# Order of work in a unit of the second attention: q in two halves, transposes and scores between the products

## What is computed

```python
kv = concat([context, latents], axis=1)          # 64 + 256 = 320 keys a batch
q = (latents @ Wq).reshape(bsz, q_len, 32, 128)  # 32 query heads
k, v = kv @ Wk, kv @ Wv                          # 8 key/value heads, 4 query heads to each
q, k = rms_norm(q, q_norm_w), rms_norm(k, k_norm_w)
scores = einsum('bhgqd,bhkd->bhgqk', qg, k) / sqrt(128)
out = einsum('bhgqk,bhkd->bhgqd', softmax(scores), v)
x = x + tanh(g_xattn[1]) * (out @ Wo)            # latents = layernorm(x)
```

## Time and profile before

| | us |
|---|---|
| median of three runs | 1485.03 (1480.28 to 1485.92) |
| the profiled execution | 1481.86 |
| its span, first to last instruction | 1480.1 |
| of it the 32 units of the second attention | 552.4 to 1412.3 |
| PE busy | 1394.9 (94%) |
| DVE busy | 1055.5 (71%) |
| ACT busy | 799.7 (54%) |
| POOL busy | 464.1 (31%) |

### The profile page before, as it was taken

The page is one execution under the profiler, slowest core; times in us unless marked ns, Lnnn a source line. Parts: engine busy times, 40 slices in busy tenths (PEclk is TensorE's granted clock), DMA queues, the critical chain, the costliest instruction groups (busy, mean ns, idle before and its releaser), DMA issues.

```text
span 1480.1 us, 24307 instructions
## 1 busy us (share of the span) xinstructions
PE 1394.9 (94%) x7976; PEld 1197.7 (81%) x7976; DVE 1055.5 (71%) x2794; ACT 799.7 (54%) x2210; POOL 464.1 (31%) x590
## 2 busy tenths in 40 slices
PE   4999999998999998999999999999999999999988
PEld 4888888897778877888878878878888888887777
DVE  7777777778632437787777777787787787787775
ACT  4777777776211315565555555555555555664642
POOL 3855555554963612111111111111121111112220
PEclk8999999999999999999999999999999999999999
DMA  4211212111321301001001001001001001010001
GB/s 192 72 62 53 71 71 71 59 69 44 105 68 43 124 1 72 1 1 72 1 1 71 0 1 71 0 1 71 0 1 71 0 1 71 0 43 13 1 8 50
DMA packets 14958, 63.96 MB, mean 43 GB/s; under 512 B 1760, under 2 KB 1760, under 8 KB 10656
## 3 DMA queue, kind: packets, MB, share of 16 engines
q1 hardware_dynamic: 14880, 63.07, 12.0%
HBM read 60.97 MB, written 2.10 MB: 43 GB/s over the span
## 4 chain that ended last, share of the span: by engine, by line
PE 39%; DVE 15%; issue 5%; ACT 4%; DVEq 0%; ACTq 0%
PE psum L57 12%; PE psum L59 11%; PE psum L58 11%; PE psum L1356 2%; PE psum L1450 2%; DVE mx L1041 2%; DVE pT_hi L1014 2%; DVE pT_lo L1010 1%; DVE w1o_lo L1003 1%; DVE p L1056 1%; DVE w1q_lo L1003 1%; ACT pT_hi L1212 1%; DVE dump L1034 1%; DVE oT_lo L1020 1%; DVE v_lo L1071 1%
## 5 line engine op out<-in xcount | busy, mean ns | idle before, releaser
L1289 ACT ACTIVATE p<-psum,nb,rq 128x320 f32<-128x320 f32 x256 | 155.2, 613 | 162.8 <-DVE nb L1045 162.8
L57 PE MATMUL psum<-w1q_hi,xnT_lo 128*128 128x512 f32 x288 | 120.9, 420 | 16.7 <-DVE v_lo L1065 9.0
L978 POOL TENSOR_TENSOR rk<-ssk,rms_eps 128x3 f32<-128x3 f32 x32 | 6.3, 196 | 350.7 <-DVE ssk L1082 350.7
L59 PE MATMUL psum<-w1q_hi,xnT_hi 128*128 128x512 f32 x288 | 113.7, 395 | 0.0
L1010 DVE TENSOR_TENSOR pT_lo<-psum,pT_hi 128x512 fp32r<-128x512 f32 x128 | 88.1, 689 | 35.9 <-ACT pT_hi L1212 34.1
L58 PE MATMUL psum<-w1q_lo,xnT_hi 128*128 128x512 f32 x288 | 112.9, 392 | 0.0
L1041 DVE TENSOR_REDUCE mx<-psum 128x2 f32<-128x640 f32 x128 | 105.0, 820 | 6.1 <-PE psum L59 0.5
L1253 ACT ACTIVATE q_raw<-psum 128x512 f32<-128x512 f32 x64 | 38.2, 597 | 123.6 <-PE psum L59 123.6
L363 DVE TENSOR_TENSOR VW_lo<-psum,VW_hi 64x512 fp32r<-64x512 f32 x128 | 88.0, 688 | 19.0 <-ACT VW_hi L459 17.4
L57 PE MATMUL psum<-w1o_hi,oT_lo 128*128 128x512 f32 x256 | 100.5, 393 | 0.0
L58 PE MATMUL psum<-w1o_lo,oT_hi 128*128 128x512 f32 x256 | 100.3, 392 | 0.0
(11 more groups left out here) (235 smaller groups left out, 4657.6 us busy)
## 6 DMA issues: line engine op xcount, KB each, us to landing
raw_q<-in_w0q SPq DMA_DIRECT2D x8, 1024.0 KB, 4.8
raw_o<-in_w0o SPq DMA_DIRECT2D x8, 1024.0 KB, 4.8
raw_q<-in_w1q SPq DMA_DIRECT2D x8, 1024.0 KB, 7.5
raw_o<-in_w1o SPq DMA_DIRECT2D x8, 1024.0 KB, 4.8
raw_kv<-in_w_gu SPq DMA_DIRECT2D x10, 512.0 KB, 3.6
raw_gu<-in_w_gu SPq DMA_DIRECT2D x10, 512.0 KB, 3.7
raw_kv<-in_w0kv SPq DMA_DIRECT2D x8, 515.0 KB, 3.3
raw_kv<-in_w1kv SPq DMA_DIRECT2D x8, 512.0 KB, 5.5
```

Source lines behind the costliest of these rows:

```text
L57: pe.matmul(out, w[1], m[0], start=start, stop=False)
L59: return pe.matmul(out, w[0], m[0], start=False, stop=stop)
L1289: last = act.activation(k.p1[:, tile, h, :], s_pair(j)[:, h % 2, :], ACT.Exp, bias=k.nb[:, i:i + 1], scale=k.rq[:, i:i + 1], accum_out=k.r ...
```

## The change

It moves work in the streams of PE, DVE and ACT, and changes two shapes:

- **q in halves by pairs of heads.** `q_proj(n, b, hp)` makes both token tiles of one pair of heads into one bank: 24 instructions of 256 columns for each half, 48 in place of 24 of 512. `q_raw` and `qT` hold the halves so; transposes, squares and splits keep their number and sizes.
- **PAIRS** goes through both tiles of heads 0 and 1 first, then of heads 2 and 3.
- **Transposes of p:** groups 0 to 2 (first pair of heads) stand in the unit itself, after score steps 2 and 3; groups 3 to 5 stay in the next unit. `p_v` comes ahead of q there.
- **Splits of weights** (`pieces`): all of `w1o` in b = 1; in b = 3 all six pieces, at new places.
- The layer-norm tiles for later phases (`ln_tiles`) and the tail follow the new order.

```diff
-    PAIRS = [(0, 0), (0, 1), (1, 0), (1, 1)]
+    PAIRS = [(0, 0), (1, 0), (0, 1), (1, 1)]
...
-        order = ["kv"] + (["cx"] if b % 2 == 0 else []) + ["q0", "q1", "pv0", "pv1", "d0", "d1"]
+        order = ["kv"] + (["cx"] if b % 2 == 0 else []) + ["pv0", "q0", "q1", "pv1", "d0", "d1"]
...
+        order = ["t3", "t4", "k", "t5", "q0", "q1", "t0", "t1", "t2"]
...
+            def q_proj(n, b, hp):
+                for tile in range(2):
+                    t = 2 * b + tile
+                    for c in range(CH):
+                        last = mm3(pe, y_bank(b, "q", hp)[:, tile * 256:(tile + 1) * 256],
+                                   [w[:, c, t * PART:(t + 1) * PART] for w in k.xnT],
+                                   [w[:, c, hp * 256:(hp + 1) * 256] for w in k.w_q], c == 0, c == CH - 1)
+                last.then_inc(q_full, 1)
...
+            def turn(u, b, j, late=False):
                 hp, kt = divmod(j, 3)
+                if j == 0:
+                    pe.wait_ge(p_scaled_pool, u + 1)
+                    pe.wait_ge(p_scaled, 3 * u + 1)
+                if j == 3:
+                    pe.wait_ge(p_scaled, 3 * u + 3)
...
+                    if prev:
+                        if b % 2 == 0:
+                            pe.wait_ge(kv_split, n + 1)
+                        p_v(u, b, 0)
+                        before = ln_tiles(u)
+                        turn(u, b, 3, late=before[1] if before else False)
+                        turn(u, b, 4)
                     if b == 0:
                         pe.wait_ge(q_wlo, CONV["q"] * (g + 1))
...
+                    if b % 2 == 0:
+                        pe.wait_ge(cx_split, 2 * g + b // 2 + 1)
+                    else:
+                        pe.wait_ge(kv_split, n + 1)
+                    q_proj(n, b, 0)
                     if prev:
+                        pe.wait_ge(t_split, 6 * u + 4)
                     pe.wait_ge(k_scaled, n + 1)
...
+                    if prev:
+                        turn(u, b, 5)
+                        pe.wait_ge(pv_split, 2 * u + 1)
+                    else:
+                        pe.wait_ge(kv_split, n + 1)
+                    q_proj(n, b, 1)
+                    pe.wait_ge(kt_split, n + 1)
+                    q_turn(n, b, 0)
+                    if prev:
+                        p_v(u, b, 1)
+                    q_turn(n, b, 1)
                     scores(n, b, 0)
                     scores(n, b, 1)
...
+                        out(u, b, 0)
                     scores(n, b, 2)
+                    turn(n, b, 0)
+                    turn(n, b, 1)
                     if prev:
+                        out(u, b, 1)
...
                     scores(n, b, 3)
+                    turn(n, b, 2, late=late[0] if late else False)
```

On DVE and ACT, in a unit's second half (`conv` is the list of weight pieces of this b):

```diff
+                    q_squares(n, 1)
+                    q_lo(n, b, 0)
+                    for c in conv[2:4]:
+                        w_lo(*c)
+                    if prev:
+                        pv_lo(u, b, 1)
+                    q_lo(n, b, 1)
                     row_max(n, 0)
                     row_max(n, 1)
                     scale_p(n, 0)
+                    if conv[4:]:
+                        w_lo(*conv[4])
+                    scale_p(n, 1)
...
+                    exps(n, 0)
+                    exps(n, 1)
+                    for c in conv[4:]:
+                        w_hi(*c)
+                    t_evac(n, b, 0)
+                    t_evac(n, b, 1)
+                    exps(n, 2)
```

More of the change, by code:

```diff
@@ L940, in weights, with pieces @@
         return raw[kind][:, s], flat[kind][0][:, s], flat[kind][1][:, s]
+    def pieces(g, b):
+        return {1: [("o", g, i) for i in range(CONV["o"])],
+                3: [("kv", g + 1, i) for i in range(CONV["kv"])] + [("q", g + 1, i) for i in range(CONV["q"])]}.get(b, [])
     def loop(eng, body, tail):
@@ L1084, in body @@
                     last.then_inc(ssk_ready, 1)
+                    if prev:
+                        t_lo(u, b, 3)
+                        t_lo(u, b, 4)
+                    dve.wait_ge(rk_ready, n + 1)
+                    for i in range(nk):
+                        last = dve.tensor_scalar(k.k_raw[:, i, :], k.k_raw[:, i, :], k.rk[:, i:i + 1], None, ALU.mult)
+                    last.then_inc(k_scaled, 1)
+                    if prev:
+                        pv_lo(u, b, 0)
                     if not nxt and b >= 2:
@@ L1090, in body @@
                         ln.dve_stats(dve, 2, 7)
[L1091 to L1102, removed]
-                        t_lo(n, b, 5)
-                    q_squares(n, b, 1)
-                    if prev:
-                        pv_lo(n, b, 0)
+                    if conv:
+                        w_lo(*conv[0])
                     dve.wait_ge(kt_hi, n + 1)
@@ new lines, in body @@
+                    if prev:
+                        t_evac(u, b, 5)
+                    if conv:
+                        w_hi(*conv[1])
+                    for late in ln_tiles(n):
+                        ln.act_norm(act, *late)
+                    q_copy(n, b, 1)
+                    q_hi(n, b, 0)
+                    for c in conv[2:4]:
+                        w_hi(*c)
+                    if prev:
+                        pv_evac(u, b, 1)
+                    q_hi(n, b, 1)
+                    exps(n, 0)
@@ L1396, in body @@
                     n, prev = BATCH * g + b, not (first and b == 0)
-                    deep = not (first and b < 2)
+                    u, deep = n - 1, not (first and b < 2)
+                    late = ln_tiles(n)
                     if b == 0:
@@ L1687, in pe_hgT @@
         if s == 0:
-            pe.wait_ge(self.free["turned"], 6 * self.units - 1)
+            pe.wait_ge(self.free["turned"], 6 * self.units)
         else:
```

338 lines of the change are left out of this document (133 added, 205 removed).

## The result

The changed kernel takes 1503.6 us, median of four runs (1501.4 to 1508.0), against 1485.5 for the kernel before (1480.3 to 1486.3): ratio 1.0135, 95% interval 1.0109 to 1.0161. It is slower, and close to the forecast of 1502. The profiled execution took 1505.1 us.

A forecast was written before the change was run, and what follows sets the result against it. PE was taken to set the time. Halves +8.3, even units -5.4, b = 1 +5.2, b = 3 +13, after jumps +2.2, ends -2.5: +21 on 1481.9 gave 1502 us, range 1487 to 1517.

The forecast's parts named there:

- the new wait: PE's eight transposes of the unit's own p wait for DVE's scaling: about 0.8, 1.5, 2.6 us (even, b = 1, b = 3).
- Q + 8.9: Even units: the p transposes start 8.9 us after PE ends q's second half (Q), 0.8 after PE is ready.
- The fifth piece: In b = 3, a weight piece on DVE between step 0's and step 1's reciprocals delays scaling step 1: +1.1 us.
- Halves +8.3: q on PE as 48 instructions of 256 columns, not 24 of 512: +0.26 us a unit, +8.3 in all, nothing hiding it.
- Even, b = 1 and b = 3 units: Time lost per unit: even 1.2 us (were 1.8), b = 1 1.75 (were 1.0), b = 3 2.85 (were 1.0).
- Behind the jump: Units after DVE's loop jump: PE stops some 2.3 us ahead of `p_v`; they lose 3.4, were 2.95; +2.2 over five.
- rival C: More places stop (context split, scaled k, first `p_v` split; perhaps PE's jump): 14 us more, 1516, up to 12 on top; chance 0.2.
- Rival D: PE's granted clock might fall after each 2.3 us stop at the jump; no term or chance of its own.
- The stop at 1039.06: Kernel before: PE's stop of about 0.7 us from p transposes whose banks wait for DVE's splits; expected to go.
- Ends: First two units +3 us, last two -2, tail -3.5: together -2.5.
- A: Chain of scaled p shorter than `out` and scores, so units lose only small gaps: faster, 1465 us; chance 0.08.
- B: DVE order right but weight pieces cost less, all odd units losing 1.2 us: about the same, 1487; chance 0.17.

## Why the prediction was right, and where it was not

- **Place and releaser of the new wait:** right. The transposes of the unit's own p wait for DVE's scaling in all 32 units, and the chain's length in even units (Q + 8.9) was right to the tenth; in b = 1 and b = 3 it ends at Q + 9.4 and 10.55, some 0.15 sooner than worked out. PE's own work to that point was taken 0.2 too short. The two together make the stops 0.58 / 1.14 / 2.25 where 0.8 / 1.5 / 2.6 were foretold.
- **The fifth piece at +1.1:** right, and shown by moving it (9.0 us of waiting less, 1.1 in each of eight b = 3 units).
- **Halves +8.3:** the pace was right, "nothing hides it" was not shown right: alone in the kernel before they cost 3. In the changed kernel no wait is left inside q, so there they may cost the whole; what they cost there was not measured apart.
- **Even, b = 1 and b = 3 units:** signs and order right, each 0.2 to 0.4 a unit too long, by the stops above and by small gaps charged too high: 7 us in all.
- **Behind the jump:** place and cause right (DVE's 2.5, no stop of PE's own, rival C not seen). The stop ahead of `p_v` is 1.85 to 2.25 where 2.3 was foretold, and the term of +2.2 with the halves, +3.5, measured +1.0 without the clock.
- **The clock:** the step that was missing. Rival D named the fall behind a stop of 2.3 us at the jump, but gave it no term in the sum ("C's size covers it") and did not see that its own b = 3 stop of 2.6 is as long. It cost 8.6 us. The unit lengths were overrated by 9.5 us. That these two cancel was luck: the forecast of 1502 is nearer to the measurement than its mechanism is. (The parts also add up to 1502.7, not 1502.)
- **The stop at 1039.06** in the kernel before, put at about 0.7, is 0.54 beyond the pace (1038.30 to 1039.06 less 0.229).
- **Ends:** the first two units cost 1.5 more than thought, the last two 1.7 more (a b = 3 stop with a fall of the clock stands there too, 0.97 in the last window), the tail was right (-3.9 against -3.5).
- **Rivals:** A fails, since PE stops ahead of the eight transposes in every unit. B fails: the fifth piece cost its 1.1, by the run in which it was moved, and odd units last 26.0 and 27.1 where B's loss of 1.2 makes 25.8.

## What to carry to other kernels

When a step is moved to where its input is fresh, count what stands in the queue of the engine that makes that input: one weight piece there, needed by nobody yet, cost 12 us, by the wait behind it and by the clock behind the wait, and one moved line gave it back. A stop taken away may only pass to the next wait behind it; here the later transposes paid in full only when the split of k and v, and then the jump back, were covered as well. And a PE stop of 2 us or more should be charged with the chance of a stretch at half clock behind it (here about one in two, at 1.4 to 1.9 us each).

## What the runs showed of the hardware

- DVE is idle for 2.3 to 2.65 us, waiting for nothing that the profile shows, at each jump back of its loop, and not at all in written-out code. PE and ACT kept their loops and have no such idle time of 1 us or more there. In the kernel before, writing DVE's groups out was worth 6 us.
- Equal stops of PE differ in whether the granted clock falls behind them: never up to 1.97 us here, 22 of 41 from 2.0 to 2.3, 9 of 10 from 3.3 on. So the total depends on more than the sum of stops: the kernel with DVE written out had fewer stops and more falls in b = 3.
- Two DVE copies of 512 elements took 0.92 us, where two subtractions of the same size (`w1q_lo` in unit 11) took 1.28.
